# Attention scores as two half-array products, every second softmax exponentiated in one pass, and the cross-attention's q and key projections as three rounded products

## What is computed

```python
# self-attention: 32 heads of 32
scores = einsum('bqhd,bkhd->bhqk', q, k) * 32 ** -0.5 + slopes * rel   # causal
probs = softmax(scores, axis=-1)
# cross-attention: 8 heads of 64; q from the normed rows, k and v from the context
qh = softmax(Wq @ q, over the 64 of a head) * 64 ** -0.5
kh = softmax(Wk @ ctx, over the row)
context = einsum('bhdn,bhen->bhde', kh, vh)
out = Wo @ einsum('bhde,bhdn->bhen', context, qh) + bo
out = out / norm(out) * g * sqrt(128)
```

## Time and profile before

| | |
|---|---|
| median of 3 runs | 3303.05 us (3302.89 to 3307.04) |
| span of the profiled execution, first to last instruction | 3299.9 us |
| median less that span (start and end around it) | 3.15 us |
| attention phase in the span | 564 to 1804 us |
| one round at full clock, one with a fall of TensorE's granted clock (5 of the 14 from one L604 to the next) | 72.35 us, 73.88 us |
| PE busy over the span | 95% |
| DVE, ACT, POOL busy over the span | 54%, 32%, 15% |

### The profile page before, as it was taken

How to read it: one execution, slowest core, us unless ns; L and a number is a source line. 1 busy time by engine, 2 the same in 40 slices (tenths; PEclk the granted TensorE clock), 3 DMA queues, 4 the chain that set the end, 5 groups by cost and what they waited for, 6 DMA issues and landing times. The chain is left out here.

```text
span 3299.9 us, 41826 instructions
## 1 busy us (share of the span) xinstructions
PE 3128.8 (95%) x15136; PEld 2393.9 (73%) x15136; DVE 1773.3 (54%) x2927; ACT 1045.8 (32%) x2356; POOL 507.1 (15%) x525
## 2 busy tenths in 40 slices
PE   7999997799999999999996799999999899999998
PEld 6888886566666666666663688888887788888887
DVE  5311112466666666666663655555555655555555
ACT  2100000566665566666651211111111211111111
POOL 2100000233333333333332100000000100000000
PEclk9999999899999999999996899999999999999999
DMA  4222223111111111111110432222122521231222
GB/s 144 93 73 75 73 70 116 41 39 38 43 46 51 38 38 39 50 38 51 38 33 31 129 82 55 76 65 75 54 82 76 153 64 54 81 81 54 62 74 78
DMA packets 83350, 218.73 MB, mean 66 GB/s; under 512 B 11984, under 2 KB 18256, under 8 KB 81232
## 3 DMA queue, kind: packets, MB, share of 16 engines
q1 hardware_dynamic: 83280, 217.78, 21.8%
HBM read 175.79 MB, written 41.94 MB: 66 GB/s over the span
## 5 line engine op out<-in xcount | busy, mean ns | idle before, releaser
L312 PE MATMUL ff_ps<-h_xT_hi,w_hi 128*128 128x512 f32 x1376 | 538.2, 391 | 13.2 <-DVE h_xT_lo L96 13.2
L312 PE MATMUL ff_ps<-h_xT_lo,w_hi 128*128 128x512 f32 x1376 | 537.1, 390 | 0.0
L312 PE MATMUL ff_ps<-h_xT_hi,w_lo 128*128 128x512 f32 x1376 | 537.0, 390 | 0.0
L1042 ACT ACTIVATE w_hi<-words 128x1024 fp32r<-128x1024 f32 x134 | 142.5, 1063 | 697.3 <-DVE words L1087 697.3
L1127 DVE TENSOR_TENSOR acc<-ff_po,acc 128x512 f32<-128x512 f32 x352 | 243.0, 692 | 210.6 <-PE ff_po L312 209.9
L312 PE MATMUL qkv_acc<-w_hi,xT_hi 128*128 128x512 f32 x768 | 300.9, 392 | 9.2 <-DVE w_lo L255 9.2
L312 PEld LDWEIGHTS ff_ps<-h_xT_hi,w_hi 128*128 128x128 f32 x1376 | 259.5, 189 | 68.3 <-issue 8.8
L312 PE MATMUL qkv_acc<-w_hi,xT_lo 128*128 128x512 f32 x768 | 299.4, 390 | 0.0
L312 PE MATMUL qkv_acc<-w_lo,xT_hi 128*128 128x512 f32 x768 | 299.3, 390 | 0.0
L312 PEld LDWEIGHTS ff_ps<-h_xT_hi,w_lo 128*128 128x128 f32 x1376 | 259.4, 189 | 54.1
L312 PEld LDWEIGHTS ff_ps<-h_xT_lo,w_hi 128*128 128x128 f32 x1376 | 259.6, 189 | 53.8
(11 more groups left out here) (156 smaller groups left out, 5305.9 us busy)
## 6 DMA issues: line engine op xcount, KB each, us to landing
words<-in_w SPq DMA_DIRECT2D x90, 512.0 KB, 3.5
qkv<-qkv_out SPq DMA_DIRECT2D x96, 256.0 KB, 2.0
words<-in_w SPq DMA_DIRECT2D x176, 128.0 KB, 4.0
sc<-in_s SPq DMA_DIRECT2D x88, 256.0 KB, 4.3
qk_in<-qkv SPq DMA_DIRECT2D x16, 1024.0 KB, 4.9
w_stage<-in_w_attn SPq DMA_DIRECT2D x56, 256.0 KB, 3.0
qkv_rows<-in_x SPq DMA_DIRECT2D x16, 512.0 KB, 3.8
ctx_in<-in_context SPq DMA_DIRECT2D x16, 512.0 KB, 3.7
```

What stands on the lines that cost most here:

```text
L312: last = nc.tensor.matmul(out, left, right, start=n == 0, stop=n == len(pairs) - 1)
L1042: nc.scalar.activation(dst, src, ACT.Copy).then_inc(s["split_hi"], 1)
```

## The change

Five things, all in the attention phase.

1. **Scores in halves.** The score product becomes two fp32 matmuls of 256 columns: rows 0 to 63 of q and of the keys (heads 0, 1 of the group) into the first bank of a new two-bank `pair_s`, rows 64 to 127 (heads 2, 3) into the second. `kD` shrinks to half. The biasing reads both halves.
2. **Sharing a bank.** `bank_q` is now the first bank of `pair_s`. So the q projection of step t waits for the biasing of step t, and the scores of t+1 wait for the subtraction of that projection. PE's order in a step becomes: scores, transposes, products with v, q projection, then as before. `m_tile` 2 and 3 go to `pair_k`, and now wait for the last copy to `kT`.
3. **Wide softmax in groups 1, 3, 5, 7** (`WIDE`): POOL adds the negated maxima to the whole group, ACT takes one exponential of 512 columns, and DVE sums the rows (in the next step) before the reciprocal.
4. **Three-term projections.** q and key projections use fp32r high and low parts: ACT and DVE split the weights once, the normed rows (`rows_high`, `rows_low`, two halves per round) and the context (`context_high`, `context_low`). The context's DMA moves to the head of the turn's list.
5. **Norms by transposes.** The eight columns of powers are spread by eight PE transposes of a broadcast column into `bank_p` and `bank_d`; the DVE diagonal is gone, and with it POOL's wait for the norms before it norms the next rows.

```diff
-    kD = sb("kD", [P, G, HG, P], F32, ph)
+    kD = sb("kD", [P, G, 2, P], F32, ph)
+    WIDE = (1, 3, 5, 7)
...
+    pair_s = pb("pair_s", [P, 2, N], ph)
+    half_s = pair_s[:, :, 0:2 * P]
+    bank_q = pair_s[:, 0, :]
+    y_banks = [pair_s[:, e, :] for e in range(2)]
+    norm_banks = [bank_p, bank_d]
...
-    m_room = [pair_o[:, D - P:D]] * 2 + [bank_s[:, 0:P]] * 2
+    m_room = [pair_o[:, D - P:D]] * 2 + [pair_k[:, N:N + P], pair_k[:, 0:P]]
...
+    def wide_sums(dve, b, t):
+        dve.wait_ge(s["s_exp"], b * G + t + 1)
+        nc.vector.tensor_reduce(row_sum[:, t, :], sc[:, t % SR, :, :], AX.X, ALU.add).then_inc(s["s_summed"], 1)
+        dve.wait_ge(s["s_summed"], wide_count(b, t))
+        nc.vector.reciprocal(row_rec[:, t, :], row_sum[:, t, :]).then_inc(s["s_rec"], 1)
...
+            if own and t < G:
+                if t == 0:
+                    pe.wait_ge(s["a_out"], 2 * b + 2)
+                    pe.wait_ge(s["kd_out"], b + 1)
+                elif cross and t > 2:
+                    pe.wait_ge(s["q_subbed"], c * KT + t - 2)
+                else:
+                    pe.wait_ge(s["s_biased"], b * G + t)
+                for e in range(2):
+                    at = slice(e * 2 * HD, (e + 1) * 2 * HD)
+                    last = nc.tensor.matmul(half_s[:, e, :], qkT[at, 0, t, :], flat(kD[at, t, :, :]), start=True,
+                                            stop=True)
+                last.then_inc(s["s_done"], 1)
...
+                    pe.wait_ge(s["xn_lo_done"], 2 * c + n // 4 + 1)
+                if own and t < G:
+                    pe.wait_ge(s["s_biased"], b * G + t + 1)
+                elif n:
+                    pe.wait_ge(s["q_subbed"], c * KT + n)
...
+                product(nc, bank_q, [(r[:, at], w[:, 0, :]) for r, w in (
+                    (xn_hi, wqk_hi), (xn_hi, wqk_lo), (xn_lo, wqk_hi))]).then_inc(s["q_done"], 1)
...
+                    last = product(nc, pair_k[:, at], [(w[:, 1, i * P:(i + 1) * P], v[:, at]) for w, v in (
+                        (wqk_hi, ctx_hi), (wqk_hi, ctx_lo), (wqk_lo, ctx_hi))])
...
                 if i == 2:
-                    pe.wait_ge(s["s_biased"], (b + 1) * G)
+                    pe.wait_ge(s["kt_out"], (b + 1) * XT)
...
-            for e, bank in enumerate(norm_banks):
-                last = nc.tensor.matmul(bank, ones[:, :], flat(diag[:, 4 * e:4 * e + 4, :]), start=True, stop=True)
+            for k in range(KT):
+                last = nc.tensor.transpose(norm_banks[k // 4][:, k % 4, :],
+                                           n_sq[:, 1, k:k + 1].to_broadcast([P, P]), ident[:, :])
...
+                if t in WIDE:
+                    act.wait_ge(s["s_subbed"], wide_count(b, t))
+                    last = nc.scalar.activation(sc[:, t % SR, :, :], sc[:, t % SR, :, :], ACT.Exp)
...
+            if own and t in WIDE:
+                pool.wait_ge(s["s_max"], b * G + t + 1)
+                nc.gpsimd.tensor_tensor(sc[:, t % SR, :, :], sc[:, t % SR, :, :],
+                                        neg_max[:, t, :].unsqueeze(2).to_broadcast([P, HG, P]),
+                                        ALU.add).then_inc(s["s_subbed"], 1)
...
-            if cross:
-                pool.wait_ge(s["r_done"], b + 1)
...
+            if own and t - 1 in WIDE:
+                wide_sums(dve, b, t - 1)
...
+            if cross and 0 < t < 3:
+                rows_low(dve, c, t - 1)
...
-            dve.wait_ge(s["n_pow"], c + 1)
-            nc.vector.tensor_tensor(diag[:, :, :], ident[:, :].unsqueeze(1).to_broadcast([P, KT, P]),
-                                    n_sq[:, 1, :].unsqueeze(2).to_broadcast([P, KT, P]), ALU.mult).then_inc(s["n_diag"], 1)
```

More of the change, by code:

```diff
@@ L520, in turn_tensor @@
                 last.then_inc(s["p_done"], 1)
[L521 to L538, removed]
             n = t - 3
@@ L599, in turn_tensor @@
             pe.wait_ge(s["d_out"], (c + 1) * KT)
-            if own:
-                pe.wait_ge(s["s_biased"], (b + 1) * G)
-            for e, bank in enumerate((bank_s, bank_q)):
+            pe.wait_ge(s["q_subbed"], (c + 1) * KT)
+            for e, bank in enumerate(y_banks):
                 for j in range(XT):
-                    last = nc.tensor.matmul(bank[:, :], z[:, j, :], qT[:, j, e * N:(e + 1) * N], start=j == 0,
+                    last = nc.tensor.matmul(bank, z[:, j, :], qT[:, j, e * N:(e + 1) * N], start=j == 0,
                                             stop=j == XT - 1)
@@ L677, in turn_scalar @@
                 nc.scalar.activation(flat(oT_hi[:, :, :]), pair_o[:, :], ACT.Copy).then_inc(s["o_hi"], 1)
+            if cross and t < 2:
+                rows_high(act, c, t)
+            if ahead and t == STEPS - 1:
+                act.wait_ge(s["k_done"], (b + 1) * XT)
+                context_high(act, b + 1)
         if cross:
             act.wait_ge(s["y_done"], c + 1)
-            for e, bank in enumerate((bank_s, bank_q)):
-                last = nc.scalar.activation(y[:, e * N:(e + 1) * N], bank[:, :], ACT.Identity, bias=bo_sb[:, 0:1])
+            for e, bank in enumerate(y_banks):
+                last = nc.scalar.activation(y[:, e * N:(e + 1) * N], bank, ACT.Identity, bias=bo_sb[:, 0:1])
             last.then_inc(s["y_out"], 1)
@@ L762, in turn_vector @@
                 nc.vector.tensor_copy(mT[:, i * P:(i + 1) * P], m_room[i]).then_inc(s["m_out"], 1)
-            if own and t < G:
+            if cross and 0 < t < 3:
+                rows_low(dve, c, t - 1)
+            if own and t < G and t not in WIDE:
                 dve.wait_ge(s["s_exp"], b * G + t + 1)
@@ L781, in turn_vector @@
                 qk_statistics(dve, b + 1)
+                context_low(dve, b + 1)
             dve.wait_ge(s["k_recced"], 2 * (b + 1))
@@ L820, in turn_vector @@
             for e, bank in enumerate(norm_banks):
-                last = nc.vector.tensor_tensor(y[:, e * N:(e + 1) * N], y[:, e * N:(e + 1) * N], bank, ALU.mult)
+                last = nc.vector.tensor_tensor(y[:, e * N:(e + 1) * N], y[:, e * N:(e + 1) * N], flat(bank[:, :, :]), ALU.mult)
             last.then_inc(s["y_scaled"], 1)
@@ L874, in _ @@
             norm_qk_affine(act, 0)
+            nc.scalar.activation(flat(wqk_hi[:, :, :]), kE[:, :], ACT.Copy).then_inc(s["wqk_hi_done"], 1)
+            context_high(act, 0)
             context_out(act, 0)
```

91 lines of the change are left out of this document (64 added, 27 removed).

## The result

| | before, same chip | changed |
|---|---|---|
| median | 3302.97 us (4 runs) | 3326.86 us (4 runs, 3323.52 to 3329.17) |
| ratio | | 1.0069, 95% interval 1.0054 to 1.0083 |
| span of the profiled execution | 3299.9 us | 3327.1 us |
| quiet round (no fall of the clock) | 72.35 us | 73.58 us |
| falls of the clock, in the 14 steps from one round's output products to the next | 5 | 12 |

The change is slower, by 24 us. The forecast was 3316.5 us with a range of 3290 to 3340. The profiled execution is the slowest of the four; the others have spans of 3321.5 to 3325.1 us.

A forecast was written before the change was run, and what follows sets the result against it. PE's list was taken to set the round, DVE's close behind, then a chain across both. Rounds +10.5, clock +9, ends -6 give +13.5 on span 3299.9; with 3.15 for the median, 3316.5 us, range 3290 to 3340.

The forecast's parts named there:

- What PE is spared: PE work saved per round by projections (2.6 us), norms (0.8) and score halves (2.7): some 6.1 us in all.
- Halves: Score product in two halves running together: 0.52 us for 0.86, so 8 x 0.34 = 2.7 us a round saved on PE.
- The shared bank: Scores, biasing, q projection and subtraction become one PE-DVE chain: even step 5.28 us, odd 5.31, pair 10.59 against 10.63.
- The walk: Step-by-step sum of instruction starts along the PE-DVE chain through a round, making the round 0.7 us longer.
- Entry: Round's start to biasing 4: first exponentials and key transposes 0.75 us sooner, step 2 5.87 us, biasing 4 unmoved.
- Exit: Biasing 7 to the output products: 15.4 us for 15.0, with 0.9 us of PE idle before `m_tile` 2 and 0.5 returned.
- the rounds' term: Each round 0.3 + 0.4 = 0.7 us longer, times 15: +10.5 us.
- The clock: Longer gap before the first key transposes makes TensorE's clock fall in 11 of 15 rounds, six more at 1.53 us: +9 us.
- one rival: Clock falls every round at the first gap (+6 us) and sometimes around step 3's first work (+9): 3331 us, chance 0.15.
- The ends: Turn 0 (-2 us) and the last turn at low clock (projections -2.4, first waits +1.3, norms -2.9): -6 us together.
- The halves do not overlap: Rival: halves fail to overlap or each shape change drains, scores 0.34 us longer, 1.1 us a round: 3332 us, chance 0.15.
- PE stays the bound: Rival: alternation looser than walked, a pair of steps takes 9.5 us, -39 us over the rounds: 3258 us, chance 0.12.

The follow-up runs named there:

- the three filled kernels: Unread fp32 products put on PE before the first key transposes: kernel before, 3293.49 us; full scores in own bank, not wide, 3269.65; halves in own banks, not wide, 3258.18.

## Why the prediction was right, and where its sizes were off

The sign, the range and the main mechanism were right: the chain through the shared bank holds the pair of steps at 10.63 us, and what PE is spared there becomes idle time in front of the q projections. PE was spared only half of what was forecast, though, and the size was off by 10 us on the median (+23.9 for +13.5). The span of the profiled execution grew by 27.2 us. By the forecast's own steps, from that execution:

- **What PE is spared.** Projections: forecast 0.70 us for three products, measured 0.81 by starts (973.79 to 974.60 in the changed kernel's step 4), of which 0.1 is lost between the first product and the second. Keys 1.41 us a step against 1.72, as forecast. Norms 0.96 against 1.72, forecast 0.93; 0.1 of it stands ahead of the score pair. **Halves: the term that was mis-sized.** 0.52 us was forecast. Measured by starts, 976.55 to 977.19, it is 0.64, and the neighbours pay too: the transposes ahead take 0.54 us to the next start and those behind 0.58. In the run with the full product in its own bank these three spaces are 0.43, 0.86 and 0.53:

```profile
897.52 0.60 PE L628 MATMUL bank_d<-ident,qr 128*128 128x128 f32 x4
897.95 1.02 PE L556 MATMUL pair_s<-kD,qkT 128*128 128x512 f32 x2
898.81 0.60 PE L566 MATMUL bank_p<-ident,scores 128*128 128x128 f32 x4
899.34 0.43 PE L579 MATMUL pair_o<-probT,v_in 128*32 128x128 f32 x8
```

  1.76 us against 1.82: a product in halves saves 0.06 us, not 0.34. Of the six microseconds forecast, PE was spared some three a round; its busy time fell by 42 us where the forecast's sign was 90, and its waits for the biasing are 0.70 to 1.35 us in the odd steps and none in steps 4 and 6, where the forecast had one in every step. The forecast weighed the Trainium skill's rule that a change of tiling mode drains the engine (TensorEngine Tiling (Array Packing), section Tiling Modes) against a row with 0.09 us. The rule was nearer: with both halves at once and free neighbours the three spaces would be 0.43 + 0.43 + 0.53 = 1.39 us, so 0.37 us are lost for each product. How much of that is drain and how much a lack of overlap, no run separates.

- **The shared bank.** Even step 5.28 forecast, 5.15 and 5.17 measured; odd step 5.31 forecast, 5.48 measured (step 3: 5.12 and 5.19); from biasing 4 to 7 there are 15.80 us for 15.55, +0.25 against a forecast of +0.3. The walk held. The odd step's excess of 0.17 us is the q projection (0.80 by starts for 0.70) and the transposes ahead of the halves (0.53 for 0.44), less small change elsewhere; DVE's even step was a little shorter.
- **Entry.** Gap before the first key transposes 2.85 forecast, 2.69 measured; biasing 4 0.1 us late for 0 forecast. What I had not seen: in step 1 the first `xn_lo` takes 1.56 us beside POOL's addition for the wide group, and biasing 2 comes 0.2 us later than walked by it; step 2 then takes 5.68 us for 5.87.
- **Exit: the step that failed.** Forecast 15.4 us, measured 15.88 (988.85 to 1004.73), before 15.0. The forecast counted `m_tile` 2's wait for the copy to `kT` (0.9, measured 0.58) and left out that in step 7 too the q projection stands behind the biasing. Before, PE began it 0.26 us ahead of biasing 7, now 0.73 us behind:

```profile
1199.33 1.02 PE L537 MATMUL bank_q<-wqk_sb,xn 128*128 128x512 f32 x2
```

  One microsecond later. 0.36 us of it comes back, since the products with v now lie ahead of the projection; the half microsecond that the shorter projections return was in the forecast already. The miss of 0.5 us in each of 15 rounds is 7 us, most of what the rounds' term (+10.5, measured 15 x 1.23 = +18.5) was short of.
- **The clock.** Forecast 11 of 15 rounds, measured 12, but three of these behind step 3's gap, as one rival had it. The price was wrong: behind the first gap a fall costs 0.8 to 1.1 us and not 1.53, because some of the slow time falls into PE's new idle time: the waits of 0.41 and 0.34 us in steps 2 and 3 are all but gone in such rounds. Behind step 3's gap it costs 1.7. The 14 steps from one L655 to the next take 1043.5 us (706.92 to 1750.46), 13.4 more than 14 quiet rounds, against 7.6 before: +5.8 for +9.
- **The ends.** Turn 0 gave -0.3 us for -2: the first key transposes of the next turn stand at 662.45, before at 662.76. The first round is 0.9 us longer than its share of the rounds' term. Last turn: first waits +3.55 for +1.3 (2.2 of it the slow `xn_lo`), projections -2.5 for -2.4, norms -2.4 for -2.9. Without that round these make about -1.6 for -6. Behind it the feed-forward phase took 3.7 us more in the profiled execution, with low clock for 44 us of it where there were 37.5; the other executions lie 2 to 5.6 us lower, so this is not the change's alone, and it stays open what of it is.
- **Rivals.** "The halves do not overlap" was right in effect: with what the neighbours lose, a product is spared 0.06 us and not 0.34. Its price of 1.1 us a round was too high: of the odd step's excess over the walk 0.1 us belongs to the halves, the rest of their miss falls into idle time. The run with the full product can't price it, since it undoes a saving of 0.06 us. "PE stays the bound" is what the kernel is with the sharing, the wide groups and the halves gone (3287 us); with the change as it is, it had no chance.

What remains as shown: the sharing costs 1.7 us a round, and the wide softmax is dearer (1.39 us) the moment that sharing goes. The rest of the change (three-term projections, norms, PE's order) holds a gain of some 16 us that these two eat up. How the 16 us divide among those three was not tried.

## What to carry to other kernels

A resource that two steps of a software pipeline come to share turns two loose waits into one chain; walk that chain through every step, the last one too, before counting what an engine is spared. When taking one suspect out brings little, take out the second with it: two waits in a row can hide each other, here 0.15 against 1.39 us. And where an engine's list is reordered, ask which idle time of it was used by what is now behind.

## What was not expected of the hardware

- **DVE beside POOL.** A DVE operation with both inputs in SBUF (128x512) took 1.56 us beside a POOL operation of 1.04 us that began 0.02 us earlier, and 2.91 us beside one of 2.34 us that began 0.02 us later; alone, and in the run that delays POOL, 0.69 us. Both times it ends about half a microsecond after POOL's operation. DVE and POOL at the shorter place, in the changed kernel:

```profile
959.17 0.69 DVE L509 SCALAR_TENSOR_TENSOR scores<-pair_s,alibi 128x512 f32<-128x512 f32 x1
...
960.69 1.56 DVE L459 TENSOR_TENSOR xn_lo<-xn,xn_hi 128x512 fp32r<-128x512 f32 x1
```

```profile
959.51 1.04 POOL L758 TENSOR_TENSOR scores<-scores,row_rec 128x512 f32<-128x512 f32 x1
960.67 1.04 POOL L763 TENSOR_TENSOR scores<-scores,neg_max 128x512 f32<-128x512 f32 x1
```

  The Trainium skill, SBUF — State Buffer, section Who interferes with whom, says that one of the two blocks until the other is done; the rows agree, by the ends. Both times DVE was the one that waited, so the two starts don't show who comes first. The biasing, with one of its inputs in PSUM, stayed at 0.69 us beside POOL's scaling.
- **Halves of the array.** Two fp32 products of 64 rows and 256 columns took 0.64 us for an ideal 0.43, and some 0.1 us more ahead of them and 0.05 behind.
- **fp32r behind fp32.** The first of three fp32r products takes 0.34 us to the next start, the others 0.23.
- **The clock.** It fell behind PE's gaps of 2.11 us in 5 of 14 rounds, behind 2.37 us in 8 to 12 of 14 and behind 2.69 us in 8 to 14 of 14, by the version. Behind the 1.35 us of step 3 it fell three times in the changed kernel and five times when the longer gap was filled. In the three filled kernels whose other gaps in a round were at most 0.44, 0.47 and 0.91 us it never fell in a round.
